# Probabilities for VectorE written over the scores in PSUM, those for GpSimd alone in SBUF

## What is computed

```python
xn  = silu(group_norm(x, gn_scale, gn_offset))            # 32 groups of 16 channels
qkv = einsum('bxyc,cd->bxyd', xn, w_qkv)
q, k, v = split(qkv, 3)                                   # 8 heads of 64 channels
sim  = einsum('bhdi,bhdj->bhij', q * HEAD_CH ** -0.5, k)  # 1024 x 1024 per head
attn = softmax(sim, axis=-1)
out  = einsum('bhij,bhdj->bhid', attn, v)
out  = einsum('bxyd,dc->bxyc', out, w_out) + b_out + x
```

## Time and profile before

| | us |
|---|---|
| median of three runs | 3793.71 |
| the profiled execution's own time | 3788.86 |
| its span, first to last instruction | 3787.1 |
| TensorE (PE) busy | 3622.2 (96%) |
| VectorE (DVE) busy | 3211.4 (85%) |
| ScalarE (ACT) busy | 2816.3 (74%) |
| GpSimd (POOL) busy | 2309.0 (61%) |

### The profile page before, as it was taken

The page is one execution under the profiler, slowest core; times in us unless marked ns, Lnnn a source line. Parts: engine busy times, 40 slices in busy tenths (PEclk is TensorE's granted clock), DMA queues, the critical chain, the costliest instruction groups (busy, mean ns, idle before and its releaser), DMA issues.

```text
span 3787.1 us, 92715 instructions
## 1 busy us (share of the span) xinstructions
PE 3622.2 (96%) x32844; PEld 2103.6 (56%) x32844; DVE 3211.4 (85%) x4027; ACT 2816.3 (74%) x3074; POOL 2309.0 (61%) x2211
## 2 busy tenths in 40 slices
PE   5899999999999999999999999999999999999997
PEld 2555555555555555555555555555555555555553
DVE  6888888888888888888888898888988888888885
ACT  3777777778777787777777777787777877777774
POOL 1383855838467494765838567494764847558444
PEclk7999999999999999999999999999999999999999
DMA  2112113132131222213132121221212222131221
GB/s 92 53 39 77 55 46 85 35 91 57 46 85 40 68 57 71 60 40 87 38 82 62 48 73 40 83 57 53 78 40 68 57 74 57 46 85 35 68 57 34
DMA packets 120776, 228.89 MB, mean 60 GB/s; under 512 B 12672, under 2 KB 29056, under 8 KB 120320
## 3 DMA queue, kind: packets, MB, share of 16 engines
q1 hardware_dynamic: 120320, 222.87, 21.9%
HBM read 71.57 MB, written 33.55 MB: 28 GB/s over the span
## 4 chain that ended last, share of the span: by engine, by line
PE 73%; DVE 14%; issue 7%; ACT 4%; DMA 1%; POOL 0%; DVEq 0%; SPq 0%; ACTq 0%; POOLq 0%
PE SD L1031 26%; PE PV L1163 14%; PE ST L1133 9%; PE ST L1134 9%; PE TP L1045 9%; DVE mx L828 5%; DVE Pl L865 3%; DVE ms L798 2%; PE TP L1052 2%; PE ST L1098 1%; ACT Ph L669 1%; PE ST L1105 1%; DVE st L842 1%; ACT th L657 1%; DVE res L781 1%
## 5 line engine op out<-in xcount | busy, mean ns | idle before, releaser
L553 POOL TENSOR_TENSOR Pl<-P,Ph 128x512 f16<-128x512 f32 x1024 | 1265.1, 1236 | 1171.6 <-ACT Ph L669 1170.5
L666 ACT ACTIVATE P<-ST,cns 128x1024 f32<-128x1024 f32 x1024 | 1141.1, 1114 | 780.0 <-PE ST L1134 767.6
L828 DVE TENSOR_REDUCE mx<-TP 128x1 f32<-128x1024 f32 x1024 | 1244.9, 1216 | 171.9 <-PE TP L1045 168.6
L669 ACT ACTIVATE Ph<-ST,cns 128x1024 f16<-128x1024 f32 x1024 | 1133.7, 1107 | 0.0
L865 DVE TENSOR_TENSOR Pl<-P,Ph 128x512 f16<-128x512 f32 x1024 | 1028.5, 1004 | 9.3 <-ACT Ph L669 6.1
L1163 PE MATMUL PV<-V,Ph 128*128 128x129 f16 (+2 forms) x10240 | 862.5, 210 | 4.4 <-POOL Pl L553 1.6
L1163 PEld LDWEIGHTS PV<-V,Ph 128*128 128x128 f16 x10240 | 771.8, 97 | 125.9 <-ACT pv_sum L677 8.9
L1163 PE MATMUL PV<-V,Pl 128*128 128x65 f16 x8192 | 835.0, 192 | 0.0
L1163 PEld LDWEIGHTS PV<-V,Pl 128*128 128x128 f16 x8192 | 723.1, 98 | 110.3 <-issue 1.1
L1134 PE MATMUL ST<-QK 128*128 128x512 f16 x2048 | 777.5, 380 | 2.6 <-issue 2.6
L1133 PE MATMUL ST<-QK 128*128 128x512 f16 x2048 | 777.6, 380 | 0.3 <-ACT Ph L669 0.2
(11 more groups left out here) (110 smaller groups left out, 3222.3 us busy)
## 6 DMA issues: line engine op xcount, KB each, us to landing
QK<-QK SPq DMA_DIRECT2D x384, 256.0 KB, 4.9
res<-in_x SPq DMA_DIRECT2D x128, 256.0 KB, 2.8
out<-res SPq DMA_DIRECT2D x128, 256.0 KB, 2.0
x_in<-in_x SPq DMA_DIRECT2D x61, 512.0 KB, 3.9
V<-V SPq DMA_DIRECT2D x16, 1040.0 KB, 6.4
V<-in_L_conv_w_qkv SPq DMA_DIRECT2D x4, 768.0 KB, 11.0
P<-in_L_conv_w_out SPq DMA_DIRECT2D x1, 1024.0 KB, 14.7
z<-in_x SPq DMA_DIRECT2D x1, 512.0 KB, 6.1
```

The lines of the kernel that those rows point to most:

```text
L553: nc.gpsimd.tensor_tensor(Pl[:, v % 4, HALF:], P32[:, v % 2, HALF:], Ph[:, v % 4, HALF:], ALU.subtract).then_inc(lo_pool, 1)
L666: nc.scalar.activation(P32[:, v % 2, :], ST[:, slot, :], ACT.Exp, scale=cns[:, 0:1])
L669: nc.scalar.activation(Ph[:, v % 4, :], ST[:, slot, :], ACT.Exp, scale=cns[:, 0:1]).then_inc(exp_done, 1)
L828: nc.vector.reduce_max(mx[:, hh, qb:qb + 1], TP[:], AX.X).then_inc(top_drained, 1)
```

## The change

ScalarE now makes three exponentials of a unit in place of two. The first writes the 16-bit `Ph` for all 1024 columns. The second writes 32 bits for the last 512 columns into `P32`, which is half as large now, and tells GpSimd through the new semaphore `exp_pool`. The third writes 32 bits for the first 512 columns over the scores themselves, in the slot of `ST`; it waits on `exp_hi`, so that the first has read them, and then raises `exp_done`. VectorE subtracts `Ph` from the slot in place of from `P32`. So a slot is in use until VectorE's low part is written, and TensorE's ring waits on `lo_dve` where it waited on `exp_done`. The staging place of the output weights moves from `P32` to `OT`, which has room before the first image.

```diff
-        P32 = sb("P32", [P, 2, 2 * HALF], F32)
+        P32 = sb("P32", [P, 2, HALF], F32)
...
             def low_probs(b, v):
-                pool.wait_ge(exp_done, UNITS * b + v + 1)
+                pool.wait_ge(exp_pool, UNITS * b + v + 1)
                 wait(pool, pv_done, UNITS * b + v - 3)
-                nc.gpsimd.tensor_tensor(Pl[:, v % 4, HALF:], P32[:, v % 2, HALF:], Ph[:, v % 4, HALF:], ALU.subtract
+                nc.gpsimd.tensor_tensor(Pl[:, v % 4, HALF:], P32[:, v % 2, :], Ph[:, v % 4, HALF:], ALU.subtract
                                         ).then_inc(lo_pool, 1)
...
                 act.wait_ge(scores_ready, UNITS * b + v + 1)
-                wait(act, lo_dve, UNITS * b + v - 1)
+                wait(act, pv_done, UNITS * b + v - 3)
+                nc.scalar.activation(Ph[:, v % 4, :], ST[:, slot, :], ACT.Exp, scale=cns[:, 0:1]).then_inc(exp_hi, 1)
+
                 wait(act, lo_pool, UNITS * b + v - 1)
-                nc.scalar.activation(P32[:, v % 2, :], ST[:, slot, :], ACT.Exp, scale=cns[:, 0:1])
-
-                wait(act, pv_done, UNITS * b + v - 3)
-                nc.scalar.activation(Ph[:, v % 4, :], ST[:, slot, :], ACT.Exp, scale=cns[:, 0:1]
+                nc.scalar.activation(P32[:, v % 2, :], ST[:, slot, HALF:], ACT.Exp, scale=cns[:, 0:1]
+                                     ).then_inc(exp_pool, 1)
+                act.wait_ge(exp_hi, UNITS * b + v + 1)
+                nc.scalar.activation(ST[:, slot, 0:HALF], ST[:, slot, 0:HALF], ACT.Exp, scale=cns[:, 0:1]
                                      ).then_inc(exp_done, 1)
...
-            def low_probs(b, v):
+            def low_probs(b, v, slot):
                 dve.wait_ge(exp_done, UNITS * b + v + 1)
                 wait(dve, pv_done, UNITS * b + v - 3)
-                nc.vector.tensor_tensor(Pl[:, v % 4, 0:HALF], P32[:, v % 2, 0:HALF], Ph[:, v % 4, 0:HALF],
+                nc.vector.tensor_tensor(Pl[:, v % 4, 0:HALF], ST[:, slot, 0:HALF], Ph[:, v % 4, 0:HALF],
                                         ALU.subtract).then_inc(lo_dve, 1)
...
                 if at < 2:
-                    wait(pe, exp_done, UNITS * b - 1 + at)
+                    wait(pe, lo_dve, UNITS * b - 1 + at)
                     return
                 kind, n = ring[at - 2]
                 if kind == "score":
-                    pe.wait_ge(exp_done, UNITS * b + n + 1)
+                    pe.wait_ge(lo_dve, UNITS * b + n + 1)
```

More of the change, by code:

```diff
@@ L169, in __init__ @@
         self.mark = dict(mark or {"qk": 0, "v": 0})
+        self.scored = 1
     def passed(self, use):
@@ L277, in conv_attention @@
             "p (c n) -> p c n", c=CC)
-        wo_stage = P32[:, :, :].rearrange("p a b -> p (a b)").rearrange("p (c n) -> p c n", c=CC)
+        wo_stage = OT[:, :, :, :].rearrange("p a c n -> p (a c n)")[:, 0:2 * CC * CH].bitcast(F32).rearrange(
+            "p (c n) -> p c n", c=CC)
         w_abs = X[:, 1, :, :].rearrange("p c n -> p (c n)").bitcast(F16)[:, 0:CC * 3 * CH].rearrange(
@@ L336, in conv_attention @@
         scores_ready = sem("scores_ready")
+        exp_hi = sem("exp_hi")
+        exp_pool = sem("exp_pool")
         exp_done = sem("exp_done")
@@ L888, in step @@
                     if not (first and v == 0):
-                        low_probs(b, v - 1)
+                        low_probs(b, v - 1, cnt.scored)
                     if v % 4 == 3 and not (first and v == 3):
@@ L893, in step @@
                         top_use(use, b + 1, cnt)
-                    cnt.next_slot()
+                    cnt.scored = cnt.next_slot()
                     turned = [(use, cnt.next_slot()) for use in unit_turn(s, u, first, last)]
@@ L1016, in _ @@
                 step(B - 1, s, 1, now, last=True)
-            low_probs(B - 1, UNITS - 1)
+            low_probs(B - 1, UNITS - 1, now.scored)
             sums(B - 1, 15)
```

## The result

The changed kernel takes 4082.41 us (median of four runs, 4079.02 to 4084.91), against 3793.19 for the kernel before, measured beside it. The ratio is 1.0761 (95% interval 1.0745 to 1.0776): 7.6% slower, where the forecast was 4047 us. The profiled execution took 4082.80, 293.9 more than that of before; the sum had +253. Its lines stand 4 to 6 lower in the file (L865 is L871, L1133 is L1139, L1105 is L1111, L1052 is L1058); L669 is `Ph` in both.

The account below looks back on a forecast made before the run. TensorE, busy 96% of the span, was taken to bound the kernel. New waits of 312.9 us less 60 of relief gave +253 on the profiled 3788.86: 4042, or 4047 us on the median; 8 times in 10, 3985 to 4105.

Parts of the forecast that it names:

- unit 1, step 0: Input turn: the next unit's scores wait for VectorE's low part behind exponentials, copy and drains; 2.51 us new TensorE idle time.
- units 3 and 7: Input turns of step 0: the next scores wait for the low part, 2.09 us each, in 15 images.
- unit 4, step 0: Turn where VectorE's L790 takes the drain's place ahead of the low part: 2.09 us, in 15 images.
- unit 9: Input turn of step 0, behind the drain of an output block that ScalarE does not touch: 2.19 us, in 15 images.
- unit 0, step 2: The turn itself waits for unit 31's low part, moving 0.48 us; with the next scores' wait 2.39 in all, 16 images.
- unit 8, step 2: The turn waits 1.88 us for unit 39's low part; with the next scores' wait 3.79 in all, in 16 images.
- unit 4, step 3: Turn taken as the mean of those in units 0 and 8 of step 2: 3.09 us, in 16 images.
- the eight, with their images: All new TensorE waits at turns: 133.2 for four input turns, 31.4 for unit 4, 148.3 for three others; 312.9 us.
- VectorE's relief: Low part no longer stretched, so L1052's shift products wait less for `ms`: 60 us gained, bounds nothing and 90.4.
- rival of a slow in-place exponential: ScalarE's third exponential takes 1.37 us in place of 0.686: 4111 us, up to 4180 possible; 8 in 100.
- rival of overlapping stalls: At three output turns the waits of turn and next scores run side by side: 48 us less, 3999; 12 in 100.
- GpSimd's earlier start: GpSimd can start 0.42 us earlier, after the second exponential; TensorE hardly waits for it, so no term in the sum.

Follow-up runs that it names:

- the ring alone: The kernel before, with only TensorE's ring wait changed from `exp_done` to `lo_dve`: 4135.04 us, ratio 1.0901.
- the runs with the order changed: The changed kernel with VectorE's low part moved ahead in its queue next to turns; moved so in ten units, 3806.81 us, ratio 1.0042.
- the run that took the two waits away: The changed kernel, with VectorE's low part first in units 2 and 10 of step 0 alone: 3974.89 us, ratio 1.0477.
- the split alone: The kernel before, with three exponentials, all to SBUF, GpSimd starting after the second, and the ring as it was: 3819.77 us, ratio 1.0070.

## Why the prediction was right, and by how much not

The sign, the place and the mechanism of the loss were right, and the time, 4082 in a range of 3985 to 4105, was 35 us above the forecast. The relief came out at its size for a reason that was only in part the one given. By its own terms:

| term | forecast, us | measured, us |
|---|---|---|
| unit 1, step 0 | 2.51 | 2.58 |
| units 3 and 7 | 2.09, 2.09 | 2.10, 2.13 |
| unit 4, step 0 | 2.09 | 2.19 |
| unit 9 | 2.19 | 1.86 |
| unit 0, step 2 | 2.39 | 2.16 |
| unit 8, step 2 | 3.79 | 3.87 |
| unit 4, step 3 | 3.09 | 3.17 |
| the eight, with their images | 312.9 | 15 x 10.86 + 16 x 9.20 = 310 |
| VectorE's relief (what is left over) | -60 | 16 x -3.55 = -57 |
| lowered clock | none | 41 to 45 |
| all (the terms add up to 294 to 298) | +253 | +294 |

*The ring.* Each price was read from two rows and one chain, and none is off by more than 0.33. The run with the ring alone, and the runs with the order changed, show that it is the wait and the queue ahead of the low part, and neither the exponential nor the read of PSUM.

*The relief.* An image takes 248.62 us in place of 229.09; without the eight places (20.06) and units 2 and 10 (3.02, below) that is 3.55 less. Units 1, 5, 9 and 13 of step 2 alone give 4.24, and there L1052's waits had been; small new waits of 0.1 to 0.4 elsewhere take some back. The reason given was the stretched low part ahead of `ms`. But in these four units `ms` itself took 0.98, 1.10, 0.98 and 0.99 us before, and takes 0.23 now: 3.1 us an image, which is most of the 4.24. Unit 1 of step 2 in the image of the earlier trace rows, before and after:

```profile
1364.19 0.98 DVE L798 TENSOR_SCALAR ms<-mx,cns 128x4 f16<-128x4 f32 x1
...
1364.00 1.15 POOL L540 TENSOR_TENSOR X<-z,X 128x512 f16<-128x512 f32 x1
```

```profile
1467.80 0.23 DVE L804 TENSOR_SCALAR ms<-mx,cns 128x4 f16<-128x4 f32 x1
...
1467.88 1.17 POOL L557 TENSOR_TENSOR Pl<-P,Ph 128x512 f16<-128x512 f32 x1 [3.50 <-ACT P L672]
```

GpSimd's operation started 0.19 ahead of `ms` before and starts 0.08 behind it now, which the prediction had not worked out; and the ring alone, whose low part still reads SBUF, has the whole 1.19 us of unit 9 and 0.56 of unit 1. So the size of the relief was in part luck. How much of it the unstretched low part is worth by itself, no run here shows.

The low part was taken at 0.68 and measures 0.681. The estimate by the fixed cycles in the Trainium skill (VectorE: DVE Perf Modes, TRN2 errata) was 0.73; the measurement decides against it here, with 0.681 from PSUM against 0.667 at best from SBUF.

*The exponentials.* In place, 0.662 us, where 0.686 was taken; to SBUF the same 512 columns take 0.681. That agrees in sign with the Trainium skill (ScalarE: Activation LUTs, Step-by-step), by 0.02 us. In the rows of unit 1 `exp_done` comes 0.13 later, where 0.16 was worked out, so the rival of a slow in-place exponential fell, with ScalarE at 72%. The sum for ScalarE's busy time was wrong: it grew by 134 us, not by 268, because the forecast added full lengths, while neighbouring exponentials overlap by 0.1 and busy time counts the overlap once; its own 0.16 a unit would have given 164. The rival of overlapping stalls fell at unit 8, where turn and scores wait one after the other.

*What failed* is a step that was not there: "what matters is when it waits". The sum priced a wait at its own length. In units 2 and 10, behind two of the eight waits, TensorE ran at the lower clock in most images, and these units cost 1.36 and 1.66 more in the mean: 3.02 an image, 45 in 15 images (41 by the run that took the two waits away). That is the 35 us and a little more. The 2.19 of unit 4 has some of it too: it is 2.07 in 12 of the 13 images, and 3.59 in image 6, behind unit 3's wait. And GpSimd's earlier start was set down as no term, which was too quick: the split alone costs 26 us by way of `ms`. In the changed kernel that term stayed small (12.8 us of waits): `ms` mostly starts just ahead of GpSimd's subtraction there, by 0.08 us in the unit shown above. That it falls so was not foreseen, and no run isolates what moved it.

## What to carry to other kernels

When a buffer is handed back by another consumer, do not ask how long that consumer's instruction takes, but what stands ahead of it in its queue at the places where the ring is tightest: here a 0.68 us subtraction held TensorE for 2 to 4 us, and order alone, eleven of them moved in an image and two exponentials swapped in eight units, turned 7.6% slower into 1.5% faster. Where a change makes TensorE wait, look at the granted clock of the stretch behind, too. And when a change shifts one engine's start by half a microsecond, look for small operations that then fall beside it.

## What the runs showed of the hardware

The clock of TensorE fell to 1.2 GHz in the middle of a kernel that keeps it busy for 91% of its span: 0.52 granted in the 3.5 us behind a wait of 2.6 us, 1.00 before. The same wait did not always bring it: behind unit 9's 2.03 us it fell in 13, 8 or 1 of 13 images, by the run. A VectorE operation on four columns, with input and output in SBUF, grew from 0.23 to 1.16 us when a GpSimd subtraction stood beside it, and ended within 0.03 us of it; VectorE's subtraction with one input in PSUM kept its 0.68 us (669 to 693 ns) in all 1024 units, in 655 of which a GpSimd operation ran beside it. The Trainium skill (SBUF — State Buffer, Who interferes with whom) tells both apart in that way: a VectorE operation with two inputs in SBUF, or in a mode that uses both ports, shares them with GpSimd, and one with a single input in SBUF, outside those modes, does not. The subtraction agrees with that. `ms` has one tensor as input, so by that rule it would have to run in such a mode; whether it does, no run here shows.
